# Second stage of a two-layer attention and experts kernel: two accumulator banks for keys, one for expert sums, and three lags moved

## The reference, cut to what matters

```python
# layer 0 (stage 1 of the kernel): group norm, softmax attention over 4096 pixels, 4 images
x = _L0_conv_ref(x, ...)
# layer 1 (stage 2 of the kernel, the one that is changed)
t = _to_tokens(x)                                  # 4 x 4096 x 128
n = _ln_t(t)
kv = silu(n @ W_kv.T).reshape(b, t, 8, 128, 2)     # 8 heads; k, v
s = einsum('hd,bthd->bth', q_proj, k)              # one score per token and head
m = cummax(s, axis=1); e = exp(s - m)
u = cumsum(e, axis=1); w = cumsum(e[..., None] * v, axis=1)
t = t + (w / u[..., None]).mean(axis=2)            # mean over the 8 heads
n = _ln_t(t)
p = softmax(n @ router_w + router_b)               # 8 experts, the best 2, shares sum to 1
t = t + sum of share * (n @ expert_w[e] + expert_b[e]) over those 2
```

## Time and profile before

| what | value |
|---|---|
| median of three runs | 2730.43 us (2727.93 to 2730.92) |
| the profiled execution | 2731.85 us, of it the span 2730.1 us |
| mean granted PE clock | 0.981 |
| PE busy | 2560.8 us (94%) |
| DVE busy | 2154.0 us (79%) |
| POOL busy | 2059.8 us (75%) |
| ACT busy | 1841.1 us (67%) |

### The profile page before, as it was taken

One profiled execution on the slowest core, in us unless ns is written; L12 is line 12 of the kernel. 1 busy time (PEld: TensorE's weight loads), 2 busy tenths in 40 slices (PEclk: granted clock), 3 DMA queues, 4 the chain that ended last, 5 costly groups with the idle time before them and its releaser, 6 DMA issues. The chain is left out here.

```text
span 2730.1 us, 37025 instructions
## 1 busy us (share of the span) xinstructions
PE 2560.8 (94%) x10851; PEld 1859.4 (68%) x10851; DVE 2154.0 (79%) x3225; ACT 1841.1 (67%) x3375; POOL 2059.8 (75%) x1688
## 2 busy tenths in 40 slices
PE   6999999999999999999999999996979999998868
PEld 2788877788887788887778888773445555555433
DVE  4788887788887788888778888861888988988984
ACT  3666777667667676667766666775877767766640
POOL 3677776777776777777677777782559989989995
PEclk7999999999999999999999999998989999999999
DMA  1000000010000010000001000101436465555645
GB/s 66 1 16 9 9 13 9 13 39 9 13 12 9 9 39 13 12 9 9 9 13 35 9 9 12 47 13 51 171 138 242 169 262 214 191 220 198 227 175 197
DMA packets 58105, 198.38 MB, mean 73 GB/s; under 512 B 12752, under 2 KB 15376, under 8 KB 40496
## 3 DMA queue, kind: packets, MB, share of 16 engines
q1 hardware_dynamic: 57904, 196.03, 20.2%
HBM read 178.04 MB, written 17.96 MB: 72 GB/s over the span
## 5 line engine op out<-in xcount | busy, mean ns | idle before, releaser
L224 POOL TENSOR_TENSOR p_lo<-pf,p_hi 128x512 fp32r<-128x512 f32 x1024 | 1319.8, 1292 | 433.6 <-ACT p_hi L502 431.0
L497 ACT ACTIVATE pf<-s_ps 128x512 f32<-128x512 f32 x1024 | 612.8, 598 | 530.6 <-PE s_ps L376 529.4
L632 DVE TENSOR_REDUCE mx<-m_ps 128x1 f32<-128x512 f32 x1024 | 703.0, 688 | 302.7 <-PE m_ps L359 298.7
L648 DVE TENSOR_TENSOR sum_ps<-sum_ps,pf 128x512 f32<-128x512 f32 x960 | 662.3, 690 | 21.0 <-ACT pf L497 20.7
L502 ACT CAST p_hi<-pf 128x512 fp32r<-128x512 f32 x1024 | 627.2, 613 | 0.0
L374 PE MATMUL s_ps<-q_hi,kd_hi 128*128 128x512 f32 x1024 | 427.5, 418 | 0.0
L359 PE MATMUL m_ps<-w_both,q_hi 128*128 128x512 f32 x1024 | 407.8, 401 | 11.2 <-DVE mx L632 5.4
L388 PE MATMUL om_ps<-p_hi,v_hi 128*128 128x512 f32 x1024 | 401.6, 392 | 4.6 <-POOL p_lo L224 4.6
L376 PE MATMUL s_ps<-q_lo,kd_hi 128*128 128x512 f32 x1024 | 399.8, 390 | 0.0
L375 PE MATMUL s_ps<-q_hi,kd_lo 128*128 128x512 f32 x1024 | 399.8, 390 | 0.0
L389 PE MATMUL om_ps<-p_hi,v_lo 128*128 128x512 f32 x1024 | 399.3, 390 | 0.0
(11 more groups left out here) (205 smaller groups left out, 3487.3 us busy)
## 6 DMA issues: line engine op xcount, KB each, us to landing
bq<-weight_rows SPq DMA_DIRECT2D x64, 1024.0 KB, 6.3
gate_b<-gate_rows SPq DMA_DIRECT2D x64, 1024.0 KB, 4.8
xb<-in_x_dram SPq DMA_DIRECT2D x8, 1024.0 KB, 6.2
rb_sb<-inverse_rows SPq DMA_DIRECT2D x32, 256.0 KB, 3.9
tokens<-xb SPq DMA_DIRECT2D x32, 256.0 KB, 2.0
tp<-tokens SPq DMA_DIRECT2D x32, 256.0 KB, 5.4
rb<-norm_rows SPq DMA_DIRECT2D x32, 256.0 KB, 5.4
tv<-tokens SPq DMA_DIRECT2D x32, 256.0 KB, 5.4
```

The costliest lines, as they stand in the source:

```text
L224: nc.gpsimd.tensor_tensor(p_lo[:, r, :], pf[:, r, :], p_hi[:, r, :].bitcast(F32), ALU.subtract).then_inc(lo_done, 1)
L497: nc.scalar.activation(pf[:, g % RING, :], s_ps[:, g % 2, :], ACT.Exp, scale=SCALE).then_inc(exp_done, 1)
L632: nc.vector.tensor_reduce(mx[:, n % 2, sub, chunk:chunk + 1], m_ps[:, j % 2, :], AX.X, ALU.max).then_inc(m_max, 1)
L648: nc.vector.tensor_tensor(sum_ps[:], sum_ps[:], p, ALU.add).then_inc(sum_done, 1)
```

## The change

Keys get two banks, used by even and odd heads in all steps; expert sums get one bank, `mo_ps`, and the odd blocks after block 26 use the first value bank, which is free by then. Product `e` moves from slot 3 + e to 4 + e. Expert `e` moves from slot 5 + e to 6 + e, but the last one shares the slot of the one before it (slot 4 of the next step holds experts 6 and 7, slot 5 none). `expert_bias` moves to slot 6 and waits for the block before to be read out. `output` moves to slot 4 of the next step, still ahead of that slot's value work. Head additions come two slots after the scan, `residual` in slot 2. The squares for the router move from slots 1 and 2 to 3 and 4, the logits from slot 3 to 5, their copy from 4 to 5, their transposition from 5 to 6. The first value no longer waits for all keys of the five blocks before.

```diff
-    V_LAG, F_LAG, G_LAG, X_LAG = 5, 11, 3, 5
+    V_LAG, F_LAG, G_LAG, X_LAG, A_LAG = 5, 11, 4, 6, 2
...
-        k_ps = psum("k_ps", [C, BANK])
+        k_ps = psum("k_ps", [C, 2, BANK])
-        mo_ps = psum("mo_ps", [C, 2, BANK])
+        mo_ps = psum("mo_ps", [C, BANK])
...
         def key_bank(k, h):
-            return v_ps[:, 1, :] if two_banks(k) and h % 2 else k_ps[:]
+            return k_ps[:, h % 2, :]
+        def sum_bank(f):
+            return v_ps[:, 0, :] if f > FREE and f % 2 else mo_ps[:]
+        def expert_slot(e):
+            return X_LAG + min(e, E - 2)
...
                 for h in range(HEADS):                       # POOL
-                    if h == 0 and stage(v - 1):
-                        add_head(v - 1, HEADS - 1)
+                    if h < A_LAG and stage(v - 1):
+                        add_head(v - 1, HEADS + h - A_LAG)
...
-                    if stage(v) and h:
-                        add_head(v, h - 1)
+                    if stage(v) and h >= A_LAG:
+                        add_head(v, h - A_LAG)
...
             def key(k, h):                                   # PE
-                after(pe, k_act, k * HEADS + h - (1 if two_banks(k) else 0))
+                after(pe, k_act, k * HEADS + h - 1)
             def value(v, h):
-                if v == 0 and h == 0:
-                    pe.wait_ge(k_act, V_LAG * HEADS)
             def expert_bias(f):
-                after(pe, out_dve, f - 1)
+                if f > FREE and f % 2:
+                    pe.wait_ge(y_dve, NBLK * HEADS)
+                after(pe, out_dve, f - 1 if f > FREE else f)
...
-                    if norm2_at(j, 1) is not None and h == 3:
+                    if norm2_at(j, 1) is not None and h == 5:
                         logits(norm2_at(j, 1))
-                    if norm2_at(j, 1) is not None and h == 5:
+                    if norm2_at(j, 1) is not None and h == 6:
                         turn_logits(norm2_at(j, 1))
-                    if stage(f - 1) and h < X_LAG:
-                        expert(f - 1, E + h - X_LAG)
-                    if stage(f) and h >= X_LAG:
-                        if h == X_LAG:
-                            expert_bias(f)
-                        expert(f, h - X_LAG)
+                    if stage(f) and h == X_LAG:
+                        expert_bias(f)
+                    for e in range(E):
+                        if stage(f) and expert_slot(e) == h:
+                            expert(f, e)
+                        if stage(f - 1) and expert_slot(e) == h + HEADS:
+                            expert(f - 1, e)
...
-                    if norm2_at(j, 1) is not None and h in (1, 2):       # ACT
-                        for b in (2 * h - 2, 2 * h - 1):
+                    if norm2_at(j, 1) is not None and h in (3, 4):
+                        for b in (2 * h - 6, 2 * h - 5):
                             square_out(norm2_at(j, 1), b)
-                    if norm2_at(j, 1) is not None and h == 4:
+                    if norm2_at(j, 1) is not None and h == 5:
                         hold_logits(norm2_at(j, 1))
...
-                    if stage(f - 1) and h == X_LAG:                      # DVE
+                    if stage(f - 1) and h == expert_slot(E - 1) - HEADS:
                         output(f - 1)
...
-                    if stage(v - 1) and h == 1:
+                    if stage(v - 1) and h == 2:
                         residual(v - 1)
```

More of the change, by code:

```diff
@@ L894, in stage @@
             return 0 <= i < NBLK
-        def two_banks(k):
-            return k < V_LAG
         def value_bank(v, h):
@@ L1169, in expert_bias @@
                 s, b, cols = place(f)
-                after(pe, out_dve, f - 1)
+                if f > FREE and f % 2:
+                    pe.wait_ge(y_dve, NBLK * HEADS)
+                after(pe, out_dve, f - 1 if f > FREE else f)
                 pe.wait_ge(gt_act, s + 1)
-                pe.matmul(mo_ps[:, f % 2, :], eb_hi[:, b, :], gt[:], start=True, stop=False)
-                pe.matmul(mo_ps[:, f % 2, :], eb_lo[:, b, :], gt[:], start=False, stop=False)
+                pe.matmul(sum_bank(f), eb_hi[:, b, :], gt[:], start=True, stop=False)
+                pe.matmul(sum_bank(f), eb_lo[:, b, :], gt[:], start=False, stop=False)
             def expert(f, e):
@@ L1179, in expert @@
                     pe.wait_ge(xg_pool, pool_gated(f, e))
-                pe.matmul(mo_ps[:, f % 2, :], ew[:, e, :], xg[:, (f * E + e) % 3, :], start=False, stop=(e == E - 1)).then_inc(x_pe, 1)
+                pe.matmul(sum_bank(f), ew[:, e, :], xg[:, (f * E + e) % 3, :], start=False, stop=(e == E - 1)).then_inc(x_pe, 1)
             for j in range(STEPS + 1):
@@ L1394, in output @@
                 tt = tv[:, f % NV, :]
-                nc.vector.tensor_tensor(tt, mo_ps[:, f % 2, :], tt, ALU.add).then_inc(out_dve, 1)
+                nc.vector.tensor_tensor(tt, sum_bank(f), tt, ALU.add).then_inc(out_dve, 1)
             def token_variance(s):
```

## The result

The changed kernel was compared with the one before three times: 2724.93 us against 2729.99 (ratio 0.9981, 95% interval 0.9973 to 0.9988), 2723.98 against 2732.07 (0.9975, 0.9963 to 0.9988) and 2724.37 against 2732.68 (0.9975, 0.9963 to 0.9986). It is faster by 5.1, 8.1 and 8.3 us, 7.2 on average, where 13.1 were forecast. The direction and the steady part came as argued; the end of the program, forecast as a gain of 2.7, is a loss of about 4.

What follows compares the result with a forecast made beforehand. No engine is full, PE has the largest share, and at most some 8 us in 98 can be had in steps 20 to 23. Terms: -13.2 + 3.3 - 0.5 - 2.7 = -13.1 us, 2717.3 against the median; range 2705 to 2731.

Steps and rivals of the forecast that it cites:

- the stretch that PE leads: From step 20's value to the end of step 21 and in like steps: two PE stops go, gaining 2.1 us each time.
- `output` ahead of the last gates: Steps 14, 18, 22, 26 and 30: `output` in slot 4 delays the last gates, costing 0.65 us each, 3.3 in all.
- One bank for sums ... hidden: Between expert 7 and `expert_bias`: `output` of 0.68 us and PE's own work in slots 5 and 6 fit in, no loss.
- POOL: nothing either way: POOL's products and head additions both move one slot, keeping their order: no gain or loss while POOL keeps up.
- The end ... sum 2.7: Last steps: 2.0 us gained from earlier gates, 0.3 lost on logits, 1.0 gained in blocks 30 and 31; range 0 to 5.
- my 1.0 for blocks 30 and 31: At the end, `output` goes first and POOL's first product has the time to itself: 0.5 us gained a block.
- A: Rival: DVE and POOL eat the gains of stretch 3, leaving 0.7 us in each of seven stretches; 2725.6 us, chance 0.16.
- stretch 3: Part of a four-step group, from 2280.39 to the end of step 21, where PE leads; 2.1 us gain claimed.
- B: Rival: `output` costs nothing in the gates' steps and half the 1.56 and 2.25 us waits count; 2704.5 us, chance 0.10.
- the two waits: PE's key waits of 1.56 us in step 20 and 2.25 in step 22, claimed only to move, without gain.
- D: Rival: waits go but the four-step group stays at 98 us, only the end gains; 2728 us, chance 0.12.
- C: Rival: DVE waits in slot 4 for experts 6 and 7, 1.5 us in each of 20 steps; 2747.3 us, chance 0.12.

## Why the prediction was right and wrong

**Right: the stretch that PE leads.** Steps 17, 21 and 25 went from 30.37 us (mean of nine) to 27.77, a gain of 2.6 for my 2.1. That little of it comes when only one stop is removed, I had not seen; for the forecast of the whole change it made no difference. DVE also decides here: where these steps are 29.2 to 29.5 us before and not 30.6, the row ahead of `residual` (L1334) took 0.43 to 0.53 us, elsewhere 0.95 to 1.58, ending with a product of POOL.

**Undersized, and for another reason: `output` ahead of the last gates.** Steps 14, 18, 22, 26 and 30 grew by 1.07 us each (21.77 to 22.84 in step 22) for my 0.65. DVE and PE there, step 22 after, against the earlier trace rows:

```profile
2319.74 0.67 DVE L1399 TENSOR_TENSOR tv<-mo_ps,tv 128x512 f32<-128x512 f32 x1
...
2324.62 0.66 PE L1135 MATMUL st_ps<-ident,g 128*128 128x128 f32 x4 [1.76 <-DVE g L1465]
```

PE stands 1.76 us for the gates where it stood 0.54: slot 5 holds no expert now, so PE is there sooner, and the gates are 1.07 later. But that is not the 0.68 of `output`. The row that grew is a small one, the difference of the two best scores (`gap`, 128x16): step 22 before, then after, then the kernel with the old logits:

```profile
2323.09 0.15 DVE L1443 TENSOR_TENSOR gap<-top 128x16 f32<-128x16 f32 x1
```

```profile
2316.02 1.66 POOL L1058 TENSOR_TENSOR acc<-acc,ay 128x512 f32<-128x512 f32 x1 [1.22 <-DVE ay L1379]
...
2316.44 1.27 DVE L1447 TENSOR_TENSOR gap<-top 128x16 f32<-128x16 f32 x1
```

```profile
2324.56 0.15 DVE L1447 TENSOR_TENSOR gap<-top 128x16 f32<-128x16 f32 x1
...
2326.75 0.67 DVE L1399 TENSOR_TENSOR tv<-mo_ps,tv 128x512 f32<-128x512 f32 x1
```

It takes 1.27 us instead of 0.15, in all fifteen such steps of the three traces, because it now stands behind the moved `residual`, beside a moved head addition of POOL that has already begun: the addition ends at 2317.68, the subtraction at 2317.71. Another row, `share` (L1449, now L1453), has shrunk from 1.30 to 0.68, which pays for `output`. In the kernel with the old logits, where `residual` and the head additions are back as well and `output` is still in slot 4, `gap` takes 0.15, `share` 0.73, and all five steps are 21.8 to 22.0 us long, as before the change. So `output` costs nothing there, and the 1.07 is the price of what was moved with `residual`, a term that my sum did not have. (That kernel takes the move of the logits back too; the three are not tested one by one.)

**Wrong: "One bank for sums ... hidden".** I set `output` against PE's slots 5 and 6 but not against what stands ahead of it on DVE in steps with `j % 4 == 0`. DVE and PE, steps 20 and 24 after:

```profile
2267.54 3.35 DVE L1360 RECIPROCAL b_r<-u_r 128x512 f32<-128x512 f32 x1
2270.81 0.63 DVE L1399 TENSOR_TENSOR tv<-mo_ps,tv 128x512 f32<-128x512 f32 x1
```

```profile
2271.49 0.50 PE L1175 MATMUL mo_ps<-gt,eb_hi 128*128 128x512 f32 x1 [2.10 <-DVE tv L1399]
...
2274.01 0.63 PE L1141 MATMUL v_ps<-xl,w_both 128*128 128x512 f32 x1
...
2368.65 0.50 PE L1175 MATMUL mo_ps<-gt,eb_hi 128*128 128x512 f32 x1 [2.08 <-DVE tv L1399]
...
2371.14 0.40 PE L1142 MATMUL v_ps<-xh,w_both 128*128 128x512 f32 x1
```

The sums and the reciprocal of slot 3 hold DVE until 2270.81, and PE waits 2.1 us. Most of it takes the place of older waits for scans. Of the twelve steps 16, 20, 24 and 28 in three traces, seven are 25.0 us long, where the kernel before has 24.8 to 25.1; in the other five PE's clock fell to 1.2 GHz after the stop, as in step 20, and they take 25.8 to 27.0. The mean is 25.44 for 24.95: 0.5 lost in each of four steps, 2.0 in all, where I had nothing, and nearly all of it is the clock's. Here too a row of DVE is stretched beside POOL: the cumulative sum ahead of the reciprocal (L1354) takes 2.32 to 2.38 us in all twelve, where before it took 1.26 in seven and about 2.4 in five. With the old logits it takes 1.64, PE stands under 0.2 us for `output` in steps 16, 20 and 24, and these steps are 24.3 us long with the same single bank.

The sum for steps 12 to 31: 7.2 forecast, less 2.1 (five gates' steps, 0.4 each) and 2.0 (four steps like 20), and 1.8 more from steps 13, 17, 21 and 25 and 0.2 from steps 12 and 29 together, is the 5.1 measured.

**Wrong: "POOL: nothing either way".** Steps 32 to 35 gained 4.1, not 1.0. Step 33 gave 2.1 of it: its stop for the squares was 1.9 us, not the average 1.27, and a wait of 1.2 to 1.6 for a product went too. In step 35 PE's waits for products, before and after:

```profile
PE mo_ps L1180 <- POOL xg L1043: 3.2, 3, 1.8
```

```profile
PE mo_ps L1183 <- POOL xg L1046: 0.4, 1, 0.4
```

The waits for products went here; I read it as the work of the head additions that come two slots late and let the products come first. No kernel tests that alone. The one with the old logits has the additions one slot late again: PE waits 2.3 us for products in its step 35, and steps 32 to 35 take 86.0 us, as before the change, which agrees but does not separate the additions from the logits.

**Wrong: "The end ... sum 2.7".** This is the step that failed, 6.7 of the error: a loss of 4.0 for a gain of 2.7. The gain I named is mostly there: PE transposes the gates 0.06 us after the last row instead of 1.7 on average (2.27, 0.58 and 2.25), 1.6 for my 2.0. Three things stand against it.

First, `output` in slot 4, which I charged in steps 14 to 30 only, also stands ahead of the gates of the drain, and there it waits for PE as well: 2.5 us, shown by the kernel that has it in slot 5.

Second, the moved logits and `residual` cost more than 0.3: the scale of the gates is ready 1.4 later. With both back in their old slots it is ready at 37.4, as before (37.2), while either alone gave 0.5 at most (38.1 and 39.3). These are single traces, and kernels that are alike up to there have 38.4 to 40.1, so how much of the 1.4 is whose stays open.

Third, my 1.0 for blocks 30 and 31 did not arrive. The first expert does come 1.33 us after the landing in block 31 (2710.77 to 2712.10) where it was 1.83 (2717.64 to 2719.47), and 1.83 it is again in both traces with `output` in slot 5 at the end. But the stretching has only moved to POOL's second product; the two together after:

```profile
2710.77 2.95 POOL L1046 TENSOR_TENSOR xg<-gate_b,tv 128x512 f32<-128x512 f32 x2 [1.95 <-DMA gate_b<-gate_rows]
```

That is 2.95 us where it was 3.00. And the second half of a block's gates is a DMA of its own, which lands about 4 us after the first in both (2721.70 and 2714.64), and `output` follows it by 5.06 us in both.
The Trainium skill, SBUF — State Buffer, section "SBUF: two separate sides", names VectorE instructions with two SBUF inputs among those that take the lock shared with GpSimd, and `output` has only one: the trace agrees so far as this row goes, since POOL's first product keeps its length beside `output`.

The rest has no test here and stays open: 0.5 us more from the transposition to the landing of block 28's gates (8.2 to 8.7), 0.5 less from there to its `output`, and 1.2 more after block 28, well inside the spread of the three traces.

That the whole sum is only 4.9 off is partly luck: steps 0 to 11 and 32 to 35 gained 3.9 us more than I had argued, against 6.7 and 2.1 less elsewhere.

**The rivals.** A's time, 2725.6, is the nearest to what was measured, but for another reason: stretch 3 did give its gain, and the end took it back. B is out, since bringing the two waits back cost nothing in their steps as long as the clock held, and so is D, since the group of steps 20 to 23 takes 97.2 us and not 98. C's mechanism is there in size (DVE waits 1.01 us for L1183 in step 23) and costs nothing, since step 23 is 20.81 us long as before:

```profile
2340.83 0.69 DVE L1399 TENSOR_TENSOR tv<-mo_ps,tv 128x512 f32<-128x512 f32 x1 [1.01 <-PE mo_ps L1183]
```

## What to carry to other kernels

A lag that is moved for the steady loop holds in the drain too: follow every moved instruction through the last steps, where nothing stands beside it, and ask what is queued behind it there. Two stops of one engine in a stretch whose end another engine or a DMA sets are one stop: price them together, since removing either alone here lengthened the other. A buffer cut from two to one turns the reader's place in its queue into a deadline; look for the longest instruction ahead of it in any step of the period, here a reciprocal of 3.35 us. And when an instruction is moved, look at what its neighbours now run beside: moving `residual` by a slot made a row of 0.15 us on DVE take 1.27, and that cost 1.07 us in every group of four steps.

## What the runs showed of the hardware

PE's granted clock makes a stop cost more than its length, and the same stop does not always cost it. In steps like 20 it fell to 1.2 GHz after an idle time of 2.10 us in one execution and stayed at 2.4 GHz after 2.08 in the same one, four steps later; the first cost 0.8 us more (25.80 against 25.01). After 1.96 us with one key bank and after 2.92 with the old logits it fell as well, but not after 1.94 and 2.93 in other steps of the same two executions, nor after 3.08 in step 28 of the changed kernel. In the kernel before it fell after 2.25 us in steps 14 and 26 and not in steps 18 and 22, and not after the stops of up to 1.54 in step 21.

DVE and POOL hold each other up. A DVE row of 128x16 that takes 0.15 us took 1.27 where a head addition of POOL had begun 0.42 us before it, and ended 0.03 us behind the addition. A cumulative sum of 1.26 us took up to 2.42, a maximum (L1334) 0.43 or up to 1.58. Two products of POOL take 2.95 to 3.00 us together where one alone takes 1.26.

Single executions of one kernel on one chip differ by 14 to 17 us of 2725 (2715.5 to 2729.4 and 2723.1 to 2740.5), while the steps between 12 and 35 repeat mostly within 0.1 us: the spread comes from the first stage and the first dozen steps (the second stage's first step begins between 1860.0 and 1863.3 us in the six traces of the two kernels), from single steps that are 0.8 to 2 us longer, and from the end.
